# One graph-network layer on one core: the experts' stage with the first expert's weights loaded ahead of the rest, another order of its first products, and two tiles to a bank in its second

## What is computed

```python
scores = ...                       # graph attention over the edges, per node and expert
topk_s, topk_i = top_k(scores, 2)
w = softmax(topk_s)
out = zeros_like(x)
for ei in range(4):
    g = where(topk_i == ei, w, 0.0).sum(-1)
    hh = gelu(x @ W1[ei] + b1[ei])          # 256 -> 512
    out = out + g[..., None] * (hh @ W2[ei] + b2[ei])   # 512 -> 256
```

## Time and profile before

| what | value |
|---|---|
| three runs, median (lowest, highest) | 2723.76 us (2709.36, 2723.77) |
| the profiled execution, its own time | 2707.9 us |
| its span, first to last instruction | 2706.1 us |
| PE busy, share of the span | 1941.8 us, 72% |
| POOL busy | 1480.2 us, 55% |
| DVE busy, ACT busy | 1194.9 us, 907.0 us |
| mean granted clock of PE | 0.827 of full speed |

### The profile page before, as it was taken

The page is one execution under the profiler, slowest core; times in us unless marked ns, Lnnn a source line. Parts: engine busy times, 40 slices in busy tenths (PEclk is TensorE's granted clock), DMA queues, the critical chain, the costliest instruction groups (busy, mean ns, idle before and its releaser), DMA issues. The chain is left out here.

```text
span 2706.1 us, 26735 instructions
## 1 busy us (share of the span) xinstructions
PE 1941.8 (72%) x7528; PEld 1341.2 (50%) x7528; DVE 1194.9 (44%) x2204; ACT 907.0 (34%) x1994; POOL 1480.2 (55%) x1512
## 2 busy tenths in 40 slices
PE   5687878876677777765455888788888788784235
PEld 4454545454455554543345555456555555553223
DVE  6353222345455555543386223324235143346368
ACT  3432444444444444443323222222323222222124
POOL 2455655666566666676602566666666666561510
PEclk9888988998888898887665899999998889897555
DMA  5443222244343434353358221212222112215544
GB/s 182 142 134 114 87 70 79 84 118 137 113 137 111 139 120 143 105 166 123 93 161 277 82 49 36 70 36 49 57 50 56 38 48 56 51 36 172 160 149 152
DMA packets 197046, 282.83 MB, mean 105 GB/s; under 512 B 43024, under 2 KB 147443, under 8 KB 195762
## 3 DMA queue, kind: packets, MB, share of 16 engines
q0 software_dynamic: 61280, 115.13, 16.6%
q1 hardware_dynamic: 97218, 121.11, 13.5%
q10 hardware_dynamic: 38416, 44.96, 5.1%
HBM read 195.29 MB, written 85.80 MB: 104 GB/s over the span
## 5 line engine op out<-in xcount | busy, mean ns | idle before, releaser
L857 POOL DMA_INDIRECT ag_msg<-xn_tab,step_src x784 | 784.8, 1001 | 462.1 <-issue 218.3
L1814 POOL DMA_INDIRECT edge_rows<-hx_d,gat_src x648 | 623.7, 962 | 357.1 <-issue 180.6
L1125 PE MATMUL ag_ps<-ag_msg,ag_hot 128*128 x1760 | 491.5, 428 | 117.4 <-issue 61.0
L2002 PE MATMUL ex_psY<-co_rows 128*128 128x256 f32 x1568 | 416.0, 426 | 130.9 <-ACT co_rows L2056 70.2
L1125 PEld LDWEIGHTS ag_ps<-ag_msg,ag_hot 128*128 128x128 f32 x1760 | 364.4, 215 | 244.2 <-issue 187.6
L879 DVE TENSOR_TENSOR acc<-acc,ag_ps 128x257 f32 x440 | 186.0, 423 | 638.3 <-remote 276.5
L2002 PEld LDWEIGHTS ex_psY<-co_rows 128*128 128x128 f32 x1568 | 332.2, 215 | 212.3 <-ACT co_rows L2056 79.9
L1990 PE MATMUL ex_psF<-co_rows 128*128 128x448 f32 x896 | 353.9, 551 | 46.2 <-DMA ex_b<-in_b_dram 24.9
L1301 ACT ACTIVATE gat_self<-iota_row,step_nloc 128x128 f32<-128x128 f32 x880 | 270.4, 388 | 304.4 <-issue 164.7
L1928 DVE TENSOR_TENSOR hi_one_low<-hi_numbers,hi_low 128x2048 bf16<-128x2048 f32 x64 | 146.4, 2287 | 498.9 <-remote 416.1
L1990 PEld LDWEIGHTS ex_psF<-co_rows 128*128 128x128 f32 x896 | 171.2, 194 | 212.5 <-issue 165.3
(11 more groups left out here) (377 smaller groups left out, 2000.0 us busy)
## 6 DMA issues: line engine op xcount, KB each, us to landing
y_d<-co_rows ACTq DMA_DIRECT2D x28, 896.0 KB
co_rows<-y_d SPq DMA_DIRECT2D x28, 896.0 KB, 9.5
ag_msg<-xn_tab,step_src POOLq DMA_INDIRECT x784
xnT<-base_d SPq DMA_DIRECT2D x7, 1792.0 KB
edge_rows<-hx_d,gat_src POOLq DMA_INDIRECT x648
base_d<-xnT ACTq DMA_DIRECT2D x7, 1024.0 KB
sums_d<-edge_rows SPq DMA_DIRECT2D x5, 1344.0 KB
xg<-in_x_dram SPq DMA_DIRECT2D x7, 896.0 KB, 5.7
```

Of the source, the lines that this page charges most:

```text
L857: pool.indirect_dma_start(msg[:, q, u, 0:D], None, c.xn_tab, bass.IndirectOffsetOnAxis(ap=t.idx[:, at:at + 1], axis=0)).then_inc(s_g[q], 16)
L1125: last = nc.tensor.matmul(bank[(at + r) % BANKS][:, 0:ROWW], hot[:, k, u0 + r * JOIN + j, :], ring[:, j * ROWW:SLOTS * ROWW][:, ds(places[ ...
L1814: pool.indirect_dma_start(G[:, j % RING, w, :], None, c.hx_d, bass.IndirectOffsetOnAxis(ap=plan.idx[:, at + w:at + w + 1], axis=0)).then_i ...
L2002: last = nc.tensor.matmul(bank[:, 0:D], hh[:, k].rearrange("p a b -> p (a b)")[:, u * P:(u + 1) * P], w2[:, e, k, :], start=(k == 0), stop ...
```

## The change

Three edits, all in the experts' part of `gat_gather_experts`. Loads: `s_w` becomes two semaphores, one for `b1` and the first expert's two matrices, one for the other three experts'; SP issues `yT`, `b1` and the first expert's matrices ahead of `hdst` and `hsrc`, and the others' behind them; PE waits for the second semaphore ahead of expert 1. First layer: output i is chunk i % 4 of half i // 4, where it was chunk i // 2 of half i % 2. Second layer: seven tiles are filled in four fills of 2, 2, 2 and 1 tiles; a fill takes one bank, ACT copies it with one instruction; the first fill waits for the first half's four Gelus alone, the second for all eight.

```diff
+        s_w = [c.sem("ex_w_first"), c.sem("ex_w_rest")]
+        FILLS = [(u, min(2, NS - u)) for u in range(0, NS, 2)]
+        WHOLE = HB // P
...
+                def weights(e):
+                    sp.dma_start(w1[:, e], a["w1"][e].rearrange("(k p) n -> p k n", p=P)).then_inc(s_w[min(e, 1)], 16)
+                    sp.dma_start(w2[:, e], a["w2"][e].rearrange("(k p) n -> p k n", p=P)).then_inc(s_w[min(e, 1)], 16)
+
+                sp.dma_start(yT, c.x2nT_d[:, :, 0:GN]).then_inc(s_yT, 16)
+                sp.dma_start(b1[:], a["b1"]).then_inc(s_w[0], 16)
+                weights(0)
                 sp.dma_start(hdst, a["gat_dst"]).then_inc(s_hin, 16)
                 sp.dma_start(hsrc, a["gat_src"]).then_inc(s_hin, 16)
-                sp.dma_start(yT, c.x2nT_d[:, :, 0:GN]).then_inc(s_yT, 16)
-                for e in range(EXPERTS):
...
+                for e in range(1, EXPERTS):
+                    weights(e)
...
             def _(pe):
                 pe.sem_inc(s_s, 1)
-                pe.wait_ge(s_w, 144)
...
-                            last = nc.tensor.matmul(psF[i % FB][:, 0:HB], w1[:, e, k, (i // 2) * P:(i // 2 + 1) * P],
-                                                    yT[:, k, (i % 2) * HB:(i % 2 + 1) * HB], start=(k == 0), stop=(k == KC - 1))
+                            last = nc.tensor.matmul(psF[i % FB][:, 0:HB], w1[:, e, k, (i % HC) * P:(i % HC + 1) * P],
+                                                    yT[:, k, (i // HC) * HB:(i // HC + 1) * HB], start=(k == 0), stop=(k == KC - 1))
...
-                    pe.wait_ge(s_ge, (g * EXPERTS + e) * NF + NF + FB)
-                    for u in range(NS):
-                        n = (g * EXPERTS + e) * NS + u
-                        bank = psY[u % YB]
-
-                        pe.wait_ge(s_yc, n + YB if u == 0 else n + 1)
-                        for k in range(HC):
-                            last = nc.tensor.matmul(bank[:, 0:D], hh[:, k].rearrange("p a b -> p (a b)")[:, u * P:(u + 1) * P],
-                                                    w2[:, e, k, :], start=(k == 0), stop=(k == HC - 1))
-                        last.then_inc(s_s, 1)
+                    for f, (u0, n) in enumerate(FILLS):
+                        if u0 == 0:
+                            pe.wait_ge(s_ge, (g * EXPERTS + e) * NF + HC + FB)
+                        elif u0 <= WHOLE < u0 + n:
+                            pe.wait_ge(s_ge, (g * EXPERTS + e) * NF + NF + FB)
+                        bank = psY[f % YB]
+
+                        pe.wait_ge(s_yc, (g * EXPERTS + e) * len(FILLS) + f + 1)
+                        for u in range(u0, u0 + n):
+                            for k in range(HC):
+                                last = nc.tensor.matmul(bank[:, (u - u0) * D:(u - u0 + 1) * D],
+                                                        hh[:, k].rearrange("p a b -> p (a b)")[:, u * P:(u + 1) * P],
+                                                        w2[:, e, k, :], start=(k == 0), stop=(k == HC - 1))
+                            last.then_inc(s_s, 1)
...
+                        if g == 0 and e < 2:
+                            pe.wait_ge(s_w[e], 32 * (EXPERTS - 1) if e else 48)
...
-                        nc.scalar.activation(hh[:, i // 2, i % 2, :], psF[i % FB][:, 0:HB], ACT.Gelu,
-                                             bias=b1[:, e * HC + i // 2:e * HC + i // 2 + 1]).then_inc(s_ge, 1)
+                        nc.scalar.activation(hh[:, i % HC, i // HC, :], psF[i % FB][:, 0:HB], ACT.Gelu,
+                                             bias=b1[:, e * HC + i % HC:e * HC + i % HC + 1]).then_inc(s_ge, 1)
...
-                    for u in range(NS):
-                        act.wait_ge(s_s, n * NS + u + 2)
-                        nc.scalar.copy(yo[:, u, :], psY[u % YB][:, 0:D]).then_inc(s_yc, 1)
-                    act.wait_ge(s_yc, n * NS + NS + YB)
+                    for f, (u0, m) in enumerate(FILLS):
+                        act.wait_ge(s_s, n * NS + u0 + m + 1)
+                        nc.scalar.copy(yo[:, u0:u0 + m, :].rearrange("p t d -> p (t d)"), psY[f % YB][:, 0:m * D]).then_inc(s_yc, 1)
+                    act.wait_ge(s_yc, (n + 1) * len(FILLS) + YB)
```

More of the change, by code:

```diff
@@ L1729, in gat_gather_experts @@
         psY = [ps(f"ex_psY{i}", [P, 512]) for i in range(YB)]
-        s_w, s_yT, s_f, s_ge, s_s, s_yc, s_yst = (c.sem("ex_" + n) for n in (
-            "w", "yT", "f", "ge", "s", "yc", "yst"))
+        s_yT, s_f, s_ge, s_s, s_yc, s_yst = (c.sem("ex_" + n) for n in (
+            "yT", "f", "ge", "s", "yc", "yst"))
+        s_w = [c.sem("ex_w_first"), c.sem("ex_w_rest")]
         NF, NS = 2 * HC, GT
+        FILLS = [(u, min(2, NS - u)) for u in range(0, NS, 2)]
+        WHOLE = HB // P
         EXPERT_UNITS = NF + NS
@@ L1739, in _ @@
                 wide = sp.value_load(plan.width[0:1, 0:1], min_val=0, max_val=1)
+                def weights(e):
[4 more added lines that the diff above has]
+                weights(0)
                 sp.dma_start(hdst, a["gat_dst"]).then_inc(s_hin, 16)
                 sp.dma_start(hsrc, a["gat_src"]).then_inc(s_hin, 16)
-                sp.dma_start(yT, c.x2nT_d[:, :, 0:GN]).then_inc(s_yT, 16)
-                for e in range(EXPERTS):
-                    sp.dma_start(w1[:, e], a["w1"][e].rearrange("(k p) n -> p k n", p=P)).then_inc(s_w, 16)
-                    sp.dma_start(w2[:, e], a["w2"][e].rearrange("(k p) n -> p k n", p=P)).then_inc(s_w, 16)
-                sp.dma_start(b1[:], a["b1"]).then_inc(s_w, 16)
+                for e in range(1, EXPERTS):
+                    weights(e)
                 def turned(g):
@@ L2040, in _ @@
                 act.sem_inc(s_yc, YB)
-                act.wait_ge(s_w, 144)
+                act.wait_ge(s_w[0], 48)
                 def expert(g, e):
```

## The result

The changed kernel takes 2695.75 us (median of 20 executions, 2657.9 to 2721.76), the kernel before 2722.23 us beside it (20 executions, 2689.3 to 2735.8). The ratio is 0.9883, with an interval of 0.9853 to 0.9913: 32 us faster, where 46 were forecast (2678).

The account below looks back on a forecast made before the run. The stage was taken as bound by PE and POOL together, through holds. Gains of 8 + 28 - 2 + 4 = 38 us took the profiled 2707.9 to 2670 us, with the median put at 2678, range 2622 to 2718.

Parts of the forecast that it names:

- The rival of the signal path: Experts' stage: PE's signals and POOL's gathers fill one path, so banks gain nothing; 2708 us as a median, chance 0.22.
- The rival in which the holds stay and only PE's waits go: Experts' stage: holds keep their length, PE's waits for copies vanish; 2623 us as a median, chance 0.18.
- the holds: Experts' stage: after 11 to 17 us of unbroken gathers PE's signals stop reaching others, until about 3 us after POOL pauses.
- The slower case: Experts' stage: holds come much sooner after a pause, POOL's pauses grow by 56 us; 2756 us, chance 0.07.
- Step 1: Stage's start: first expert's weights loaded first bring PE's first product 11.3 us sooner; 8 us taken as gain.
- Step 2: Second layer: two tiles to a bank let PE run four tiles in a hold; 28 us gained.
- The balance: Experts' stage: cycle of PE's work, POOL's gathers and 3 us pauses; 6.88 us of banks cut pauses by 31 us.
- if PE's idle only moves to other lines: Experts' stage: a sign, named beforehand, that the prediction is wrong; no size given.
- Step 3: Second layer's copies on ACT: 196 become 112, those of 512 columns taken at 0.7 us; 2 us lost.
- Step 4: Second layer's start: waits for four Gelus instead of eight; 4 us gained, upper bound 15.3 us.
- Step 5: After the experts: next loads and transposes follow the last expert, so the stage's gain goes to the end.
- The clock: PE's granted clock in the experts' stage: a mean of 0.91 before, forecast over 0.93 after the change.

Follow-up runs that it names:

- h2_half_gathers: The changed kernel with every second of the 648 gathers left out, on a chip with holds: 2488.12 us beside 2725.37 us for the kernel before, one execution.
- i1_single: The changed kernel with one tile to a bank again, on a chip with holds: 2665.08 us against 2682.79 us for the kernel before, ratio 0.9923.
- i2_lead14: The changed kernel with POOL allowed 14 units ahead of PE's progress instead of 7, on a chip with holds: 2664.95 us, ratio 0.9926 to the kernel before.
- h1_no_loads: The changed kernel with the old order of loads under one semaphore, on a chip with holds: 2703.13 us, ratio 0.9956 to the kernel before.
- e4_all_gelus: The changed kernel with the second layer's first fill waiting for all eight Gelus, on the chip without holds: 2249.14 us, ratio 0.994 to the kernel before.
- f1_after: The changed kernel, unedited, on the chip without holds: 2258.93 us against 2261.28 us for the kernel before, ratio 0.9983.
- f2_before: The kernel before, unedited, on the chip without holds, run for its trace: 2260.51 us.

## Why the prediction was right, and where it was off

**The direction** was right, and so was the cause of the loss. Faster, within the range. The loss of the stage goes with the gathers, as h2_half_gathers shows. How the change gains was right for the start and not for the banks, and that the total came out near the forecast is in part luck, as the steps show. The rival of the signal path (2708) lies above the whole interval of the ratio, which at before's 2723.76 is 2684 to 2700, and with the start at its measured 12 us it would still say 2704. That margin is thin, and the rival's mechanism, a path that gathers and signals share, stays open. What the prediction cites for it from the Trainium skill (NOTIFIC — the notification-queue block, section Overflow: three behaviours, one of which stalls the engine) is said there of notification records, not of semaphore signals or gathers, so it supports this rival less than the prediction took it to. The rival in which the holds stay and only PE's waits go (2623) lies 61 us below it. The slower case didn't come: POOL's pauses fell from 176.5 us in all to 142.2.

**Step 1, the start.** PE's first product came 12.2 us sooner against the first load, where 11.3 were worked out and 8 taken. The loads behind the first expert's took no share that mattered. Whether POOL's pause at the start came back as a later hold, as the prediction feared, no trace shows. DVE's columns came 4.0 us later, not 5.5, and cost nothing that the traces show. This term was 4 us too small. It holds on all three chips: 8.2 to 9.3 us from the first load to the first product in every kernel with the new loads, 19.9 to 21.4 in those with the old.

**Step 2, two tiles to a bank.** This is the step that failed: 28 us, less 2 for the copies. The runs give it 11 us, uncertain by 13 and across two chips, and nothing, uncertain by 10, on the one chip where i1_single and i2_lead14 stand side by side. The balance let PE use all 6.88 us of its banks in a hold. The timeline of after shows it crawling past the first bank, and the groups, against i1_single, show 44.5 us less of waiting for copies but only 7.3 less of idle in all. I had named this as what would make me wrong ("if PE's idle only moves to other lines"), and for most of it that is what happened. POOL's idle beyond issue fell by 34 us, near the forecast 31, but it isn't proof of the balance, since i1_single has it as low without the banks. The balance also wanted fewer holds, and the waits of ACT's copies called remote don't show that: 32 in after, 27 in h1_no_loads, and 27 in before. The stretch came to 953 us where some 930 were forecast, and the waits for copies to 40 where 15 were.

**Step 3, the copies.** 84 copies of 512 columns took 0.58 us each, not 0.7, and 28 of 256 took 0.37. The 2 us were, if anything, too many.

**Step 4, half after half.** The waits for Gelus, 15.3 us before, are 14.4 in after, so they didn't go. e4_all_gelus, on the chip without holds, isn't seen to lose by waiting for all eight. What i1_single gains, 0.77% or 21 us, less the 12 of the start, leaves 9 us for the order, uncertain by 10. How the gain beyond the start divides between banks and order stays open. It is 20 us as 32 less 12, and 12 us in h1_no_loads (1 to 23). Each part's own interval holds zero; only the sum is measured as more than nothing.

**Step 5** held. From the next stage's first load to the end it is 243.6 us in after and 244.3 in before.

**The clock** was forecast over 0.93 and is 0.92. Most of the idling moved rather than went: 159 us before, 147 after. Where it did go, in h2_half_gathers, with 8 us of idle, the granted clock went to 1.00. By the Trainium skill (TensorE: Matmul & The Clock Gate, section Why this matters for your kernels) idle gaps between bursts bring the clock down, and these rows agree with it.

In sum 38 us were forecast and 32 measured (26 by the medians of all executions): 4 too few for the start, some 15 too many for the banks, and the rest within what the runs can tell. Two errors of opposite sign partly cancel in it. The forecast of 2678 added 8 us for a profiled execution at the low edge of its runs; before's median was 2722 in 20 executions, 14 above that execution, so this allowance was 6 us short.

## What to carry to other kernels

When an engine waits for something that the profile can't name, leave out half the work of the engine beside it before spending on more buffers: one execution of h2_half_gathers sized the whole loss, 217 us, where the buffers touched some 11, and perhaps none. A buffer that removes 44 us of one wait is worth what the engine's idle loses in all, so add up every line of that engine. And a ratio measured on one chip needn't hold on the next: the same change is 1.2% on one and not measurable on another, because what bounds the stage isn't the same.

## What the hardware showed that I had not expected

- Three chips, one program: 2261, 2683 and 2725 us. The holds are on the second and third (36 waits called remote at ACT's copies in i1_single) and absent on the first (none in f1_after or f2_before), at the same 956 to 968 ns for a gather. I had read "11 to 17 us of gathers bring a hold" as the way of the machine; it depends on the chip. Why is open.
- Half the gathers save 217 us of the experts' stretch on a chip with holds. On the chip without them they bring the experts' stretch to 735.4 us, from 742.3, and there only move the end from the gathers to PE.
- The next stage's products, which crawled beside gathers in the earlier trace rows, run at full rate beside the same gathers on the fast chip. From PE's timeline of f2_before:

```profile
2113.79 8.71 PE L2178 MATMUL gc_ps_in<-gc_carry,lane_hot 128*128 128x25 f32 x40
2122.33 6.58 PE L2178 MATMUL gc_ps_out<-gc_carry,lane_hot 128*128 128x25 f32 x30
```
